# First head's attention laid beside the last pair of expert value heads

## The chip, the cores and the metric

The kernel runs on one core of a Trainium2 chip. The metric is device time in microseconds (us). The kernel before takes 1966.53 us (median of 3 runs, 1964.88 to 1967.22). The engines are TensorE (PE; its weight loads are PEld), VectorE (DVE), ScalarE (ACT), GpSimd (POOL) and SyncE (SP), which here only issues DMAs.

## The reference

Two layers on x of 32 sequences of 100 tokens and 256 channels (3200 tokens). The first is a gated cross-attention. The second, which the change touches, is a Switch-head layer: 8 heads, and in each 8 experts for the values and 8 for the output, of which a token uses 2.

```python
q = jnp.einsum('bsd,hpd->bhsp', x, q_w.reshape(H, P, D))
k = jnp.einsum('bsd,hpd->bhsp', x, k_w.reshape(H, P, D))
xv = jnp.einsum('bsd,hedp->bshep', x, v_w.reshape(H, E, D, P))
v = jnp.einsum('bshep,bshe->bhsp', xv, gate_v)
att = jax.nn.softmax(jnp.einsum('bhqp,bhkp->bhqk', q, k) * SCALE, axis=-1)
ctx = jnp.einsum('bhqk,bhkp->bqhp', att, v)
weighted = ctx[:, :, :, None, :] * gate_o[..., None]
out = jnp.einsum('bshep,hepd->bsd', weighted, o_w.reshape(H, E, P, D))
```

H = 8 heads, E = 8 experts, P = 128 channels of a head, D = 256, attention within each sequence of 100 tokens. Everything is float32; the kernel makes the large products from float16 high and low parts (hi·hi, hi·lo, lo·hi), so that each takes three matmuls.

## The kernel before, in words

Three stages follow each other: queries, cross-attention, and the expert stage (from about 600 us on), which is one block of programs, one for each engine. Engines run their own lists in order and meet at semaphores. The expert stage has four phases.

**Gates and q, k.** The layer-normalised x is turned and split into `xhi`, `xlo`; the gates are computed; q and k of all heads are written to the DRAM tensor `qk` (until about 757 us).

**Values.** Four pairs of heads, 25 tiles of 128 tokens each, two units (`unit`, one for each head of the pair) per tile: 200 units. A unit is 12 matmuls of 512 columns (L1226) in two halves of 6, each half into one bank of `e_pv`. VectorE gates and sums the first half (four operations at L1104 and L1108, then the sum `e_dsum` at L1115), ScalarE gates the second half (four operations, L1165), GpSimd adds it all (L994, L998, L1002) into `e_out`. TensorE may fill a half's bank again when the unit before last has been read: `s_ds` for the first half, `s_av` for the second. SyncE stores five tiles at a time to the DRAM tensor `v` (L954). The last stores are waited for at L967.

**Attention of head 0 alone** (`attention_alone`). A group is 4 sequences, 400 tokens; a head has 8. For group b: scores (TensorE, L1599), maxima (VectorE, L1465, L1469), exponentials (ScalarE, L1548), reciprocal (L1475), normalisation (GpSimd, L1431). In the next group's turn: the turning of the weights (TensorE, L1608), its copy (VectorE, L1480), the product with v (TensorE `attend`, L1617), and the split of the result into `a_chi` (ScalarE, L1555) and `a_clo` (VectorE, L1484). In the same phase SyncE loads the output weights of head 0 in four pieces (L1381), x1 into `o_main` (L1385), q, k and v of each group (L1362, L1363, L1373); ScalarE and VectorE split the pieces (`piece`, L1581 and L1517), GpSimd clears `o_side` (L1455).

**Heads** (`heads`). Output tiles of head h (L1637: 12 matmuls of 512 columns each, three tiles to a group, a 25th tile at a head's end) lie beside the attention groups of head h+1. So group 8 here is the first group of head 1, beside the first three output tiles of head 0. Within a group TensorE does scores of b, the turning of b-1, a tile, `attend` of b-1, two tiles. Behind the first group of each two, one weight piece of the next head is split: ScalarE waits there for the DMA of the piece (`o_wst`), VectorE for ScalarE. SyncE's loop loads, for each two groups, q and k of the next, v, again q, k, v, and then one piece.

```python
def attention_alone(eng, group, piece=lambda h, buf, jj: None):
    for jj in range(2):
        group(fixed(jj), ())
        piece(0, 0, 2 * jj)
        piece(0, 0, 2 * jj + 1)
    with eng.Fori(1, NGR // 2) as jj:
        group(Batch(2 * jj, 0, jj), ())
        group(Batch(2 * jj + 1, 1, jj), ())
```

Of the kernel before, what the change touches and what calls it, by code (L numbers as in the profile page):

```python
# [29 lines left out]
P = 128  # L30
# [842 lines left out]
def stage_experts_in(nc, k, sems, big, mv, sel_t, q_t, k_t, v_t, rs, qk_out, v_out):  # L873


    with ExitStack() as ctx:
# [6 lines left out]
        xhi, xlo = (m.sbuf(f"e_x{n}", [P, DC, T], F16) for n in ("hi", "lo"))  # L883
        std, rstd, half = (m.sbuf(n, [SQ, NB]) for n in ("e_std", "e_rstd", "e_half"))
        wst = m.sbuf("e_wst", [P, 2, DC, H * PD])
        sst = m.sbuf("e_sst", [P, DC, P])
        shi, slo = (m.sbuf(f"e_s{n}", [P, DC, P], F16) for n in ("hi", "lo"))
        qkhi, qklo = (m.sbuf(f"e_qk{n}", [P, DC, 2 * H * PD], F16) for n in ("hi", "lo"))
        vhi, vlo = (m.sbuf(f"e_v{n}", [P, DC, HE * PD], F16) for n in ("hi", "lo"))
# [4 lines left out]
        order = m.sbuf("e_order", [P, E])  # L894
        rsb = m.sbuf("e_rs", [P, 1])
        m1, m2, top, tot = (m.sbuf(f"e_{n}", [P, NT * 2 * H]) for n in ("m1", "m2", "top", "tot"))
# [53 lines left out]
        def sync_values(sp, between):  # L950
            def stores(i):
                for g in range(5):
                    sp.wait_ge(s_vo, 50 * i + 10 * (g + 1) + 2)
                    sp.dma_start(  # L954
                        v_out[640 * g:640 * g + 640, bass.ds(i * 2 * PD, 2 * PD)].rearrange(
                            "(t p) n -> p t n", p=P),
                        vout[:, 5 * g:5 * g + 5, :, :].rearrange("p t a d -> p t (a d)")
                    ).then_inc(s_vst[g], 16)

            with sp.Fori(0, H // 2 - 1) as i:  # L960
                stores(i)
            for g in range(5):
                sp.wait_ge(s_vst[g], 16 * 2)
            between(sp)
            stores(H // 2 - 1)
            for g in range(5):
                sp.wait_ge(s_vst[g], 16 * (1 + H // 2))  # L967

        def gpsimd(pool):
# [35 lines left out]
            with pool.Fori(0, H // 2) as i:  # L1005
                for g in range(5):
                    pool.wait_ge(s_vst[g], 16 * i + 16)
                    pass_wait(pool, s_pass)
                    with pool.Fori(5 * g, 5 * g + 5) as t:
                        unit(i, g, t, 0)  # L1010
                        unit(i, g, t, 1)

        def vector(dve):
# [67 lines left out]
            for h in range(H):  # L1081
                cut = slice(h * E * PD, (h + 1) * E * PD)
                dve.wait_ge(s_vw[h % 2], 16 * (h // 2 + 1))
                dve.tensor_scalar(vhi[:, :, cut], wst[:, h % 2, :, :], WS, None,
                                  ALU.mult).then_inc(s_vhi, 1)
                dve.wait_ge(s_vhi, h + 1)
                dve.scalar_tensor_tensor(out=vlo[:, :, cut], in0=wst[:, h % 2, :, :], scalar=WS,
                                         in1=vhi[:, :, cut], op0=ALU.mult,
                                         op1=ALU.subtract).then_inc(s_vlo, 1)
# [28 lines left out]
            with dve.Fori(0, H // 2) as i:  # L1118
                with dve.Fori(0, NT) as t:
                    unit(i, t, 0)  # L1120
                    unit(i, t, 1)

        def scalar(act):
# [44 lines left out]
            with act.Fori(0, H // 2) as i:  # L1168
                with act.Fori(0, NT) as t:
                    unit(i, t, 0)  # L1170
                    unit(i, t, 1)

        def tensor(pe):
# [42 lines left out]
            def unit(i, t, hh):  # L1216
                n = 50 * i + 2 * t + hh
                for half in range(2):
# [4 lines left out]
                    col = 2 * E * PD * i + E * PD * hh + half * 512  # L1223
                    for j, (c, a, b) in enumerate((c, a, b) for c in range(DC)
                                                  for a, b in ((xhi, vhi), (xhi, vlo), (xlo, vhi))):
                        last = pe.matmul(p_v[:, hh, half, :], a[:, c, bass.ds(t * P, P)],  # L1226
                                         b[:, c, bass.ds(col, 512)], start=j == 0, stop=j == 3 * DC - 1)
                    last.then_inc(s_vp, 1)

            with pe.Fori(0, H // 2) as i:  # L1230
# [3 lines left out]

        programs = Programs()
        programs.sync, programs.sync_values, programs.gpsimd = sync, sync_values, gpsimd
        programs.vector, programs.scalar, programs.tensor = vector, scalar, tensor
        programs.s_gates = s_go
# [3 lines left out]
def stage_attention_out(nc, k, sems, experts, x1, qk, v, o_w, y):  # L1242
# [42 lines left out]
    def attention_alone(eng, group, piece=lambda h, buf, jj: None):  # L1285

        for jj in range(2):
# [42 lines left out]
    with ExitStack() as ctx:  # L1330
# [45 lines left out]
        def sync_second(sp):  # L1376
            load_v(sp, fixed(0))
# [415 lines left out]
```

## Time and profile before

| quantity | value |
|---|---|
| median of 3 runs | 1966.53 us |
| the profiled execution's own time | 1965.53 us |
| its span, first to last instruction | 1963.7 us |
| busy: TensorE, VectorE, ScalarE, GpSimd | 96%, 77%, 58%, 48% of the span |
| last expert matmul starts | 1276.14 us |
| first output matmul (L1637) starts | 1325.92 us |

A busy share is the union of an engine's instructions over the span. Matmuls overlap in the records: their starts, not their lengths, tell how fast they follow one another. The granted clock is the share of TensorE's full clock, 2.4 GHz, that it had; 0.5 is 1.2 GHz. A line of a timeline has start, length, engine, line, operation, output and inputs, count, and in square brackets the idle time ahead of it with what ended it.

### The profile page before, as it was taken

How to read it: one execution, taken by the hardware profiler on the slowest of the kernel's cores; microseconds unless marked ns; L12 is line 12 of the kernel's file. 1: busy time of each engine (PE TensorE's matmuls, PEld its weight loads, DVE VectorE, ACT ScalarE, POOL GpSimd, SP SyncE). 2: the span in 40 equal slices, each digit the busy share in tenths (PEclk: the TensorE clock that was granted, in tenths of full speed). 3: DMA queues.
4: the chain of work that ended last, by engine and by line, in shares of the span. 5: the costliest groups of instructions: out<-in, count | busy, mean ns of one | idle time of the engine just before them, and what ended most of it. 6: DMA issues, size and time to landing. Idle time of an engine off the chain costs nothing. (4 is left out here: it accounts for less than half of the span.)

```text
span 1963.7 us, 59110 instructions
## 1 busy us (share of the span) xinstructions
PE 1885.1 (96%) x13454; PEld 1154.2 (59%) x13454; DVE 1503.7 (77%) x4285; ACT 1138.9 (58%) x3588; POOL 933.8 (48%) x1361
## 2 busy tenths in 40 slices
PE   5899999999997999999999999959999999999998
PEld 2678888888875554444444444455555555555543
DVE  6688898888987943555555555538999999999989
ACT  3688888888885444444444444435555555555543
POOL 4122222222212003666666666626677766766767
PEclk9999999999998999999999999969999999999999
DMA  3777888788752483000000000063222222222202
GB/s 123 145 115 117 118 119 120 119 119 121 119 80 104 204 332 130 27 27 27 27 27 27 27 24 20 27 191 91 72 78 72 68 83 66 79 73 76 76 10 68
DMA packets 192136, 174.08 MB, mean 89 GB/s; under 512 B 51921, under 2 KB 183378, under 8 KB 190034
## 3 DMA queue, kind: packets, MB, share of 16 engines
q1 hardware_dynamic: 189906, 165.06, 37.0%
q0 software_dynamic: 2176, 8.39, 1.2%
q8 instruction: 23, 0.38, 0.1%
q14 instruction: 31, 0.25, 0.1%
HBM read 112.41 MB, written 60.98 MB: 88 GB/s over the span
## 5 line engine op out<-in xcount | busy, mean ns | idle before, releaser
L1442 POOL TENSOR_TENSOR o_side<-o_side,o_tmp 128x256 f32 (+1 forms) x528 | 398.4, 755 | 193.0 <-POOL o_side L1442 73.3
L1165 ACT ACTIVATE big<-e_pv,gates 128x128 f32<-128x128 f32 x800 | 228.7, 369 | 291.4 <-PE e_pv L1226 289.9
L640 ACT ACTIVATE c_ex<-c_sm,c_nmax 100x361 f32<-100x361 f32 x512 | 302.6, 593 | 55.5 <-DVE c_nmax L523 50.1
L1565 ACT ACTIVATE o_tmp<-o_py,gates 128x256 f32<-128x256 f32 x528 | 222.3, 475 | 191.9 <-PE o_py L1637 141.4
L1637 PE MATMUL o_py<-o_whi,a_chi 128*128 128x512 f16 x800 | 304.1, 380 | 0.4 <-DVE o_side L1498 0.2
L1226 PE MATMUL e_pv<-e_vhi,e_xhi 128*128 x800 | 303.2, 379 | 1.2 <-ACT e_out L1155 1.2
L1637 PE MATMUL o_py<-o_wlo,a_chi 128*128 128x512 f16 x800 | 303.5, 379 | 0.0
L1637 PE MATMUL o_py<-o_whi,a_clo 128*128 128x512 f16 x800 | 303.4, 379 | 0.0
L1226 PE MATMUL e_pv<-e_vlo,e_xhi 128*128 x800 | 303.2, 379 | 0.0
L1226 PE MATMUL e_pv<-e_vhi,e_xlo 128*128 x800 | 303.2, 379 | 0.0
L1104 DVE TENSOR_SCALAR e_acc<-e_pv,gates 128x128 f32<-128x128 f32 x400 | 121.8, 346 | 236.3 <-PE e_pv L1226 236.3
L523 DVE CUSTOM_DVE_ANT_0 c_sm<-c_ps,c_mbias 100x361 f32<-100x361 f32 x512 | 268.6, 526 | 39.9 <-PE c_ps L725 33.0
L1498 DVE SCALAR_TENSOR_TENSOR o_main<-o_py,gates,o_main 128x256 f32 (+1 forms) x536 | 256.0, 478 | 36.1 <-issue 20.8
L1498 DVE SCALAR_TENSOR_TENSOR o_side<-o_py,gates,o_side 128x256 f32 (+1 forms) x536 | 254.0, 474 | 0.0
L732 PE MATMUL c_pt<-ident,c_ex 100*121 100x100 f32 x1536 | 244.8, 268 | 3.6 <-ACT c_ex L640 1.8
L732 PEld LDWEIGHTS c_pt<-ident,c_ex 100*121 100x121 f32 x1536 | 215.3, 185 | 28.7 <-DVE c_ext L533 6.8
L994 POOL TENSOR_TENSOR big<-big 128x256 f32<-128x256 f32 x200 | 145.1, 726 | 159.2 <-ACT big L1165 112.7
L479 POOL TENSOR_SCALAR c_mbias<-c_mraw 100x361 f32<-100x361 uint8 x32 | 15.9, 497 | 391.2 <-DMA c_mraw<-in_mask 239.8
L725 PE MATMUL c_ps<-c_kst,c_qst 128*100 128x361 f16 x512 | 171.9, 336 | 7.5 <-DVE c_nmax L523 2.8
L533 DVE COPY c_ext<-c_pt 121x300 f32<-121x300 f32 x320 | 148.4, 464 | 8.1 <-PE c_pt L732 7.2
L1548 ACT ACTIVATE a_ex<-a_ps,a_mxs 100x100 f32<-100x100 f32 x256 | 84.8, 343 | 110.6 <-DVE a_mxs L1469 110.6
L1226 PEld LDWEIGHTS e_pv<-e_vhi,e_xhi 128*128 x800 | 78.3, 98 | 95.9 <-issue 1.6
(166 smaller groups left out, 3392.4 us busy)
## 6 DMA issues: line engine op xcount, KB each, us to landing
qk<-e_out SPq DMA_DIRECT2D x16, 1600.0 KB, 5.2
c_kst<-k_parts SPq DMA_DIRECT2D x256, 90.2 KB, 4.9
a_q<-qk SPq DMA_DIRECT2D x64, 200.0 KB, 2.4
a_k<-qk SPq DMA_DIRECT2D x64, 200.0 KB, 2.5
v<-e_out SPq DMA_DIRECT2D x20, 640.0 KB, 3.3
a_v<-v SPq DMA_DIRECT2D x64, 200.0 KB
c_ctx<-in_ctx_t SPq DMA_DIRECT2D x32, 361.0 KB, 3.4
e_wst<-in_v_w POOLq DMA_DIRECT2D x8, 1024.0 KB, 7.8
```

What stands on the lines that cost most here:

```text
L523: dve.tensor_tensor_reduce(out=sm[:, h % 4, :], in0=p_s[0:SQ, h % 2, 0:SK], in1=mbias[:, b.par, :], scale=-0.25 / WS, scalar=BIG, op0=ALU. ...
L533: dve.tensor_copy(ext[:, h % RING, :], p_t[0:KW, h % 2, 0:KC * SQ]).then_inc(s_extd, 1)
L640: act.activation(ex[:, h % 4, 0:SK], sm[:, h % 4, :], ACT.Exp, scale=-1.0, bias=nmax[:, h % 4:h % 4 + 1], accum_out=den[:, b.par, HEAD[h]: ...
L725: pe.matmul(p_s[0:SQ, h % 2, 0:SK], qst[:, b.par, HEAD[h], :], kst[:, b.par, HEAD[h] // 2, :], start=True, stop=True).then_inc(s_s, 1)
L732: last = pe.transpose(p_t[0:KW, h % 2, c * SQ:(c + 1) * SQ], ex[:, h % 4, c * KW:(c + 1) * KW], k.ident[0:SQ, 0:SQ])
L994: pool.tensor_tensor(tsum[:, hh, :, :], tmp[:, hh, 0:2, :], tmp[:, hh, 2:4, :], ALU.add).then_inc(s_ts, 1)
L1165: act.activation(tmp[:, hh, e, :], p_v[:, hh, 1, e * PD:(e + 1) * PD], ACT.Copy, scale=gate).then_inc(s_av, 1)
L1226: last = pe.matmul(p_v[:, hh, half, :], a[:, c, bass.ds(t * P, P)], b[:, c, bass.ds(col, 512)], start=j == 0, stop=j == 3 * DC - 1)
L1442: pool.tensor_tensor(side[:, x.t, :], side[:, x.t, :], tmp[:, slot(x, r), j, :], ALU.add).then_inc(s_pool, 1)
L1498: dve.scalar_tensor_tensor(out=into[:, x.t, :], in0=p_y[:, q, j, :], scalar=gate, in1=into[:, x.t, :], op0=ALU.mult, op1=ALU.add).then_inc ...
L1565: act.activation(tmp[:, slot(x, r), j, :], p_y[:, q, j, :], ACT.Copy, scale=gate).then_inc(s_av, 1)
L1637: last = pe.matmul(p_y[:, q, :, :].rearrange("p j d -> p (j d)"), a[:, bass.ds(buf * T + x.t * P, P)], b[:, buf, cut], start=j == 0, stop= ...
```

## The change

Every engine's program of the expert stage runs only three of the four pairs in its loop. The fourth is handed out as `last_pair(t)`, one tile's two units, written out without a loop. `first_head` takes the place of `attention_alone`: it lays three of these tiles into each of the 8 groups of head 0, in the places where the heads have output tiles, and tile 24 behind them. The value weights stand in one tensor `e_vw`, hi and lo of two heads together, so that the pairs that are done free room; `o_main`, `o_side` and others are placed over dead tensors. The pieces of head 0's output weights are loaded ahead of the values, x1 in the last pair. GpSimd clears `o_side` in eight parts. Ahead of the heads TensorE waits until VectorE and ScalarE have read the last unit. SyncE issues the last stores among the groups' loads, and waits for the last one ahead of the loads of head 1.

```diff
-            with pe.Fori(0, H // 2) as i:
+            with pe.Fori(0, H // 2 - 1) as i:
                 with pe.Fori(0, NT) as t:
                     unit(i, t, 0)
                     unit(i, t, 1)
 
+            def last_pair(t):
+                unit(H // 2 - 1, t, 0)
+                unit(H // 2 - 1, t, 1)
+
+            return last_pair
...
-    def attention_alone(eng, group, piece=lambda h, buf, jj: None):
-
-        for jj in range(2):
-            group(fixed(jj), ())
-            piece(0, 0, 2 * jj)
-            piece(0, 0, 2 * jj + 1)
-        with eng.Fori(1, NGR // 2) as jj:
-            group(Batch(2 * jj, 0, jj), ())
-            group(Batch(2 * jj + 1, 1, jj), ())
+    def first_head(eng, group, last_pair, piece=lambda h, buf, jj: None):
+
+        for b in range(NGR):
+            group(fixed(b), [(lambda t=t: last_pair(t)) for t in range(TT * b, TT * b + TT)])
+            if b < 2:
+                piece(0, 0, 2 * b)
+                piece(0, 0, 2 * b + 1)
+        last_pair(NT - 1)
...
         def sync_first(sp):
             load_qk(sp, fixed(0))
             load_qk(sp, fixed(1))
+            for jj in range(PIECES):
+                load_piece(sp, 0, jj)
...
+            load_v(sp, fixed(0))
+            load_v(sp, fixed(1))
             load_qk(sp, fixed(2))
-            load_v(sp, fixed(1))
-            load_x1(0)
-            load_x1(1)
-            with sp.Fori(1, NGR // 2) as jj:
-                groups(0, jj)
-                load_x1(jj + 1)
+            for g in range(5):
+                load_x1(g)
+            stored = 0
+            for b in range(2, NGR):
+                load_qk(sp, fixed(b + 1))
+                load_v(sp, fixed(b))
+                while 5 * (stored + 1) < TT * b + 1:
+                    store_values(stored)
+                    stored += 1
+            while stored < 5:
+                store_values(stored)
+                stored += 1
+            for g in range(5):
+                sp.wait_ge(experts.s_values_stored[g], 16 * (1 + H // 2))
             with sp.Fori(1, H - 1) as h:
...
-            def clear(h, buf, jj):
-                if jj == 2:
-                    pool.memset(side[:, :, :], 0.0).then_inc(s_pool, POOL_AHEAD)
-
-            attention_alone(pool, group, clear)
+            CLEARED = TT * (NGR - 1)
+
+            def beside(t):
+                last_pair(t)
+                if t % TT == 1 and t < CLEARED:
+                    pool.memset(side[:, t - 1:t - 1 + TT, :], 0.0).then_inc(s_clear, 1)
+
+            first_head(pool, group, beside)
+            pool.memset(side[:, CLEARED:NT, :], 0.0).then_inc(s_pool, POOL_AHEAD)
...
-            attention_alone(pe, group)
+            first_head(pe, group, last_pair)
+            pe.wait_ge(experts.s_gated_dve, 2 + NT * H)
+            pe.wait_ge(experts.s_gated_act, 8 + 4 * NT * H)
             heads(pe, group, tile, lambda h, buf, jj: None, rest)
```

How the instructions stand on TensorE, from the end of the value loop into head 0. Before (`a_ps` are scores, `a_pt` the turned weights, `a_pc` the product with v):

```order
L1231 COMPARE_AND_BRANCH
L1230 REGISTER_ALU
L1230 COMPARE_AND_BRANCH
L1599 MATMUL a_ps<-a_k,a_q 100x100 x8
L1608 MATMUL a_pt<-ident,a_ex 100x100 x4
L1617 MATMUL a_pc<-a_ext,a_v 128x100 x4
L1291 UNCONDITIONAL_BRANCH
```

Now, the start of a middle group (`e_vw` are the value weights; two units follow, then `a_pc`):

```order
L1637 MATMUL a_ps<-a_k,a_q 100x100 x4
L1646 MATMUL a_pt<-ident,a_ex 100x100 x4
L1244 MATMUL e_pv<-e_vw,e_xhi 128x512 x2
L1244 MATMUL e_pv<-e_vw,e_xlo 128x512
...
L1655 MATMUL a_pc<-a_ext,a_v 128x100 x4
```

The scores of a group stand ahead of its first tile and `attend` of the group before stands behind it; 72 expert matmuls now lie between one group's scores and the next's, where there were none.

How TensorE goes over into the heads now. The branch carries the two new waits:

```order
L1244 MATMUL e_pv<-e_vw,e_xlo 128x512
L1349 UNCONDITIONAL_BRANCH [waits e_s_av,e_s_ds]
L1341 UNCONDITIONAL_BRANCH
L1341 ISA
L53 ISA [waits a_s_k_0,a_s_q_0]
L1637 MATMUL a_ps<-a_k,a_q 100x100 [waits a_s_ex]
```

Scores of group 8 stand behind tile 24 of the last pair and behind both waits; before, scores of group 8 stood behind `attend` of group 6.

SyncE's queue at the same place, before (the last five stores, then everything for head 0):

```order
L1373 DMA a_v<-v 100x4x128 [waits e_s_vst_3,e_s_vst_4,e_s_vst_2,e_s_vst_0,e_s_vst_1]
L954 DMA v<-e_out 128x5x256 [waits e_s_vo] x5
L1381 DMA o_wst<-in_o_w 128x512 [waits e_s_vst_3,e_s_vst_2,e_s_vst_4,e_s_vst_1,e_s_vst_0]
L1381 DMA o_wst<-in_o_w 128x512 x3
L1362 DMA a_q<-qk 128x400 [waits a_s_s]
L1363 DMA a_k<-qk 128x400
L1373 DMA a_v<-v 100x4x128
L1385 DMA o_main<-x 128x5x256 x2
```

and now (the last two stores, the wait for all, then the loop of head 1 with its first piece `o_wst` behind q, k, v, q, k, v):

```order
L955 DMA v<-e_out 128x5x256 [waits e_s_vo] x2
L1444 UNCONDITIONAL_BRANCH [waits e_s_vst_3,e_s_vst_2,e_s_vst_4,e_s_vst_1,e_s_vst_0]
...
L1388 DMA a_q<-qk 128x400
...
L1389 DMA a_k<-qk 128x400
...
L1392 DMA o_wst<-in_o_w 128x512
```

The wait for the last store moved from ahead of head 0's loads to ahead of head 1's.

## Rows read from the trace of the kernel before

**Rows 1.** The page, part 2: 40 slices of 49.1 us, TensorE and its granted clock.

```profile
PE   5899999999997999999999999959999999999998
...
PEclk9999999999998999999999999969999999999999
```

**Rows 2.** Busy time by engine in two stretches (windows).

```profile
core 0: us, PE busy (x) PEld busy (x) DVE busy (x) ACT busy (x) POOL busy (x), PEclk, DMA share, GB/s
1275.00:1300.00 25.00, 7.83 (x48) 6.33 (x45) 9.60 (x20) 8.32 (x28) 10.29 (x9) 0.61 0.60 186
1300.00:1325.00 25.00, 20.01 (x115) 18.46 (x116) 10.13 (x28) 11.51 (x54) 5.06 (x7) 0.64 0.59 181
```

**Rows 3.** Timeline of TensorE, last expert matmuls to scores of group 10.

```profile
1262.11 0.38 PE L1226 MATMUL e_pv<-e_vhi,e_xhi 128*128 x1
...
1276.14 0.38 PE L1226 MATMUL e_pv<-e_vhi,e_xlo 128*128 x1
1276.35 1.57 PE L1599 MATMUL a_ps<-a_k,a_q 128*100 128x100 f32 x16
1281.79 0.90 PE L1608 MATMUL a_pt<-ident,a_ex 100*100 100x100 f32 x4 [3.87 <-POOL a_ex L1431]
...
1335.73 0.87 PE L1599 MATMUL a_ps<-a_k,a_q 128*100 128x100 f32 x8
...
1345.83 0.34 PE L1599 MATMUL a_ps<-a_k,a_q 128*100 128x100 f32 x2
```

**Rows 4.** Timeline of TensorE, one full group in the heads.

```profile
1407.04 0.87 PE L1599 MATMUL a_ps<-a_k,a_q 128*100 128x100 f32 x8
1407.74 0.51 PE L1608 MATMUL a_pt<-ident,a_ex 100*100 100x100 f32 x4
...
1416.73 0.87 PE L1599 MATMUL a_ps<-a_k,a_q 128*100 128x100 f32 x8
```

**Rows 5.** Timeline of VectorE, an expert unit of the last tile.

```profile
1275.46 0.61 DVE L1104 TENSOR_SCALAR e_acc<-e_pv,gates 128x128 f32<-128x128 f32 x2 [0.98 <-PE e_pv L1226]
...
1276.76 0.29 DVE L1115 TENSOR_TENSOR e_dsum<-e_acc 128x128 f32<-128x128 f32 x1
```

**Rows 6.** Timeline of ScalarE, the last expert unit.

```profile
1276.72 1.14 ACT L1165 ACTIVATE big<-e_pv,gates 128x128 f32<-128x128 f32 x4 [1.35 <-PE e_pv L1226]
```

**Rows 7.** Timeline of GpSimd, last expert units, first normalisation, clearing of side.

```profile
1276.98 0.46 POOL L1002 TENSOR_TENSOR e_out<-e_tsum,e_dsum 128x128 f32 x1 [0.18 <-POOL e_tsum L998]
...
1279.46 0.45 POOL L1002 TENSOR_TENSOR e_out<-e_tsum,e_dsum 128x128 f32 x1 [0.18 <-POOL e_tsum L998]
1280.88 0.85 POOL L1431 TENSOR_TENSOR a_ex<-a_ex,a_rsum 100x400 f32<-100x400 f32 x1 [0.97 <-DVE a_rsum L1475]
...
1294.64 5.43 POOL L1455 MEMSET o_side<- 128x6400 f32 x1
```

**Rows 8.** Timeline of the DMA issues on SyncE's queue.

```profile
1279.94 0.37 SPq L954 DMA_DIRECT2D v<-e_out  x1
1283.63 1.78 SPq L1381 DMA_DIRECT2D o_wst<-in_o_w  x4
...
1331.01 0.31 SPq L1373 DMA_DIRECT2D a_v<-v  x1
1331.80 0.35 SPq L1381 DMA_DIRECT2D o_wst<-in_o_w  x1
```

**Rows 9.** DMA issues in the heads: count, size, us from issue to landing.

```profile
a_k<-qk SPq DMA_DIRECT2D x45, 200.0 KB, 2.4
o_wst<-in_o_w SPq DMA_DIRECT2D x24, 256.0 KB, 3.1
```

**Rows 10.** Timeline of ScalarE, the first weight piece of head 1.

```profile
1336.29 0.63 ACT L1581 ACTIVATE o_whi<-o_wst  x1
```

**Rows 11.** Timeline of VectorE behind that piece.

```profile
1338.48 0.58 DVE L1480 COPY a_ext<-a_pt 100x400 f32<-100x400 f32 x1
```

**Rows 12.** Timeline of TensorE, the attention product it waits for.

```profile
1339.37 1.03 PE L1617 MATMUL a_pc<-a_ext,a_v 100*128 100x100 f32 x8
```

More of the change, by code:

```diff
@@ L948, in sync, with sync_values, store @@
             sp.wait_ge(s_vlo, H)
-        def sync_values(sp, between):
-            def stores(i):
-                for g in range(5):
[L953 to L961, printed above, removed]
+        def sync_values(sp):
+            def store(i, g):
+                sp.wait_ge(s_vo, 50 * i + 10 * (g + 1) + 2)
+                sp.dma_start(
+                    v_out[640 * g:640 * g + 640, bass.ds(i * 2 * PD, 2 * PD)].rearrange(
+                        "(t p) n -> p t n", p=P),
+                    vout[:, 5 * g:5 * g + 5, :, :].rearrange("p t a d -> p t (a d)")
+                ).then_inc(s_vst[g], 16)
+            with sp.Fori(0, H // 2 - 1) as i:
+                for g in range(5):
+                    store(i, g)
             for g in range(5):
                 sp.wait_ge(s_vst[g], 16 * 2)
[L964 to L967, printed above, removed]
+            return lambda g: store(H // 2 - 1, g)
         def gpsimd(pool):
@@ L1011, in gpsimd @@
                         unit(i, g, t, 1)
+            def last_pair(t):
+                if t % 5 == 0:
+                    pool.wait_ge(s_vst[t // 5], 16 * (H // 2))
+                unit(H // 2 - 1, t // 5, t, 0)
+                unit(H // 2 - 1, t // 5, t, 1)
+            return last_pair
         def vector(dve):
@@ L1171, in scalar, with last_pair @@
                     unit(i, t, 1)
+            def last_pair(t):
+                unit(H // 2 - 1, t, 0)
+                unit(H // 2 - 1, t, 1)
+            return last_pair
         def tensor(pe):
@@ L1233, in tensor, with last_pair @@
                     unit(i, t, 1)
+            def last_pair(t):
+                unit(H // 2 - 1, t, 0)
+                unit(H // 2 - 1, t, 1)
+            return last_pair
         programs = Programs()
@@ L1519, in piece @@
                                          op1=ALU.subtract).then_inc(s_wlo, 1)
-            attention_alone(dve, group, piece)
+            first_head(dve, group, last_pair, piece)
             dve.wait_ge(s_g, 1)
+            dve.wait_ge(s_clear, NGR - 1)
             dve.wait_ge(s_x, 80)
@@ L1581, in piece @@
                 act.activation(whi[:, buf, cut], wst[:, cut], ACT.Copy, scale=WS).then_inc(s_whi, 1)
-            attention_alone(act, group, piece)
+            first_head(act, group, last_pair, piece)
             act.wait_ge(s_g, 1)
@@ L1590, in scalar, with tensor @@
             heads(act, group, tile, piece, rest)
-        def tensor(pe):
+        def tensor(pe, last_pair):
             def scores(b):
```

91 lines of the change are left out of this document (44 added, 47 removed).

## The prediction

> **What bounds the kernel now.** I read the page's 40 slices first. TensorE has a 9 nearly everywhere; the dip that lies in the expert stage is slice 26, with a 5 and a granted clock of 6 [rows 1]. The table by windows puts it between 1275 and 1325 us: TensorE is busy for 7.83 and 20.01 of 25 us, at 0.61 and 0.64 of its clock [rows 2]. That is the attention of head 0, alone. On both sides TensorE is the bound: 65 expert matmuls start between 1262.11 and 1276.14, one each 0.2158 us without a gap [rows 3], and in the heads two groups start 9.69 us apart [rows 4], of which 36 output matmuls at 0.2158 are 7.77. So the time of a change here is read on TensorE, from the first scores at 1276.35 to a point that both kernels pass in the same state. I take the scores of group 10 at 1345.83: 69.48 us, by way of group 9 at 1335.73 [rows 3]. In it lies the work of head 0's attention and of six output tiles.
>
> **What the attention costs beside other work.** A group in the heads is 9.69 − 7.77 = 1.92 us of TensorE: scores 0.70 (1407.04 to 1407.74), turning and product with v 1.22 together [rows 4]. Before the heads begin, the changed kernel has 8 scores and 7 of the other two beside the last pair: 8·0.70 + 7·1.22 = 14.1 us. Then the waits must be covered.
> TensorE may run ahead by a unit, as each half has its own bank. Of 2.59 us for a unit (12·0.2158), VectorE needs 1.6 (1275.46 to 1276.76 + 0.29) and idled 0.98 ahead of it [rows 5]; ScalarE needs 1.14 and idled 1.35 [rows 6]. A group adds to VectorE a maximum and a copy (0.58 for the copy, [rows 11], and I take as much for the others) for some 2 us, against six units' idle time of 6·0.98 = 5.9 and the 1.92 that the group itself makes longer. It adds to GpSimd a normalisation of 0.85 us and a share of the clearing, 5.43·3/25 = 0.65 [rows 7]. To ScalarE it adds four exponentials, for which I take the 1.14 of a gating. All find room within one or two units, and a unit's lag is what the banks allow. Followed through one group, with TensorE's scores at 0: copy of the turned weights done at about 2.1, gating of the first half (ready at 2.4) by 3.9, exponentials by 3.0, second half (ready at 3.7) by 4.9; the bank is wanted again for it from 8.4 on. The load of the table for exponentials, once, and the pieces of head 0 fit too: each stands behind a whole group's room. I cost all these waits at nothing; bounds from 0 to 1.5 us for each of 8 groups (a whole unit of VectorE that TensorE waits for), so 0 to 12, and nothing below. Code without loops has fewer register instructions, but TensorE is bound by its matmuls already, so no gain there.
> VectorE's last sum of a unit ran from 1276.76 to 1277.05. A GpSimd addition started within it, at 1276.98, and took 0.46; the one at 1279.46, with no such sum beside it, took 0.45 [rows 5, 7]. So the two do not hold each other up for longer than a row shows.
> The Trainium skill, in "SBUF — State Buffer", section "Who interferes with whom", says that a VectorE instruction with two SBUF inputs and a GpSimd instruction that reads SBUF take turns, the second waiting until the first is done; a clearing, which only writes, is spared. By it the addition at 1276.98 should have waited until 1277.05, which the trace does not bear out, and a normalisation could hold up VectorE's sum once a group.
>
> **The step into the heads.** TensorE now waits for the last gating. ScalarE's ended at 1276.72 + 1.14 = 1277.86, 1.51 us after TensorE was free at 1276.35 [rows 3, 6]. With an answer of some 0.15 that is 1.65 us of idle TensorE, between 0.5 (had it been ready) and 3.0 (ScalarE a unit's work late). Then scores of group 8 to scores of group 9: 9.69. GpSimd's last part of the clearing, 5.43·4/25 = 0.87 us, starts 3.6 us after 1276.35 [rows 7] and ends at 4.4; VectorE's first output gating could start near 3.9. I cost this at nothing, as the banks of three more products lie between; bound 0.7.
>
> **The wait that is next.** SyncE issues the last store when GpSimd is done, at 1279.94, and issued the next DMA at 1283.63, its landing waited for [rows 8]. That is 7.28 us after 1276.35. Now this wait stands ahead of the loads of head 1. Counted from the scores of group 8 (1.65 later) the first of them goes out at 5.6. The piece of head 1 stands behind six other loads: the spacing between two issues that wait for nothing is 0.79 (1331.01 to 1331.80), so 4.7, and its landing takes 3.1 [rows 8, 9]: 5.6 + 4.7 + 3.1 = 13.4. ScalarE wants it 0.56 after the scores of group 9 (1336.29 against 1335.73), so at 9.69 + 0.56 = 10.25 [rows 3, 10]. It is 3.2 us late. Behind ScalarE's split stand on VectorE its own split, the maxima and the copy, which ended at 1339.06 where TensorE's product with v started at 1339.37 [rows 11, 12]: 0.3 of slack. TensorE stands still for 2.9 us in group 9, which was 10.10 long before, now 13.0. The q and k of group 9 go out at 6.4 and land 2.4 later, at 8.8, in time for 9.69. Bounds: nothing, if SyncE's issues go closer together and the piece lands with its neighbours; 5.5, if it takes 1.5 more to land and the loop 1 more to enter.
> The clock: transposes that started after an idle 3.87 us took 0.90 for four, against 0.51 at the full clock [rows 3, 4]. A halt of 2.9 may do the same to what follows. A granted clock of 0.5 over a few us costs about half of them; I take 0.5, bounds 0 and 1.7.
>
> **The sum.** 14.1 + 1.65 + 9.69 + 13.0 + 0.5 = 38.9 us, where there were 69.48. 30.5 us go. The profiled execution's own time is 1965.53, its span 1963.7 and 1.8 around it; it comes to 1935.0. The median of the runs is 1.0 above that execution: 1936.0. What stays the same: pairs one to three and heads 1 to 7, in which TensorE's order is unchanged. x1 loads beside the last pair and head 0's pieces ahead of the values, both long before anything waits for them.
>
> **Rivals.**
> 1. The piece of head 1 comes in time. Group 9 keeps its 10.10: 14.1 + 1.65 + 9.69 + 10.10 = 35.5, 34.0 go: 1932.5. For it: the landings are medians, and some issues follow each other faster. Against it: 3.2 us are a lot to find in seven issues. Chance 0.17.
> 2. Forecast, 1936, own range 1933.5 to 1940. Chance 0.60.
> 3. The last pair is not free of halts: the banks' lag of a unit is used up when a group's additions fall on VectorE, ScalarE and GpSimd together. At 1.5 us for each of 8 groups 12 more: 1948. To it belongs also, as its smaller case, that the normalisation holds up VectorE's sum for its whole length in each group: 8·0.85 = 6.8, 1943. The rule of the Trainium skill above stands for that case; I give it 0.03 of the chance here. For it: GpSimd is the last in the chain, with three additions a unit. Against it: in the heads TensorE keeps its 9.69 with the same attention beside it. Chance 0.18.
> 4. Slower. The attention's chain queues behind units: an exponential behind ScalarE's gating, the normalisation behind GpSimd's chain, the copy behind VectorE's unit; if TensorE reached the turning before this chain ended, it would wait in each group for a unit's way through three engines, from 1275.46 to 1279.91, 4.5 us [rows 5, 7]; 8·4.5 = 36: 1972. It decides from 30.5/8 = 3.8 us a group on. Against it: the turning is a whole group, 15.5 us of expert matmuls, behind the scores. Chance 0.03.
> 5. The change doesn't do what it says: head 0's work is held back by a load or a buffer until the last pair has ended, and the time stays within 0.2% (4 us, about what runs of this kernel can tell from none). Chance 0.02.
>
> **Numbers.** The likeliest is 1936. 1 to 3 together make 0.95. The range goes from just below the first rival to about the shared-access case of the third, 1931 to 1946, which leaves out most of 3's upper half and the last two, some 0.15. Faster by over 0.2%: 0.95; within: 0.02; slower: 0.03.
>
> **What would show it.** Right: in the last pair expert matmuls keep 0.2158 us apart with the attention's between; groups start 17.5 us apart (72 matmuls, 15.54, and 1.92); the granted clock is 1.00 in it; a gap of 1.65 us ahead of group 8; ScalarE idle ahead of its first split of head 1 with the DMA named, and TensorE idle for about 3 us at the product with v in group 9. Wrong: halts of TensorE at `e_pv` named after `e_dsum` or `big`; a late q or k in group 9; a group 9 as long as the others.

## The result, and the profile after

| | before | changed |
|---|---|---|
| median, us (runs) | 1965.70 (4) | 1935.82 (4) |
| lowest to highest | 1963.51 to 1967.22 | 1932.65 to 1941.85 |
| profiled execution: time / span | 1965.53 / 1963.7 | 1935.28 / 1933.5 |
| granted clock, mean | 0.984 | 0.995 |
| TensorE busy | 1885.1 | 1873.0 |

The changed kernel takes 0.9853 of the time before, with a 95% interval of 0.9837 to 0.9869. The medians are 29.9 us apart. The prediction said 1936.0, in a range of 1931 to 1946.

The page of the changed kernel, part 2, answers to [rows 1] (40 slices, of 48.3 us now):

```profile
PE   5999999999997999999999999999999999999998
...
PEclk9999999999998999999999999999999999999999
```

The dip at slice 26 is gone: TensorE has a 9 there, and so has the granted clock. The timeline of TensorE in the last pair of heads of the value experts, one group of head 0's attention:

```profile
1162.10 0.87 PE L1637 MATMUL a_ps<-a_k,a_q 128*100 128x100 f32 x8
1162.81 0.51 PE L1646 MATMUL a_pt<-ident,a_ex 100*100 100x100 f32 x4
...
1168.34 1.03 PE L1655 MATMUL a_pc<-a_ext,a_v 100*128 100x100 f32 x8
...
1179.57 0.87 PE L1637 MATMUL a_ps<-a_k,a_q 128*100 128x100 f32 x8
```

From scores to scores are 17.47 us, and the row at 1162.81 shows the full clock (0.51 for four transposes, where [rows 3] had 0.90). The granted clock from 1145.86 to 1289.69 is 1.00. No row of TensorE between 1145.86 and 1289.69 names a wait.

The timeline of TensorE from the last groups into the heads, which answers to [rows 3, 12]:

```profile
1266.88 0.87 PE L1637 MATMUL a_ps<-a_k,a_q 128*100 128x100 f32 x8
...
1289.30 0.38 PE L1244 MATMUL e_pv<-e_vw,e_xlo 128*128 128x512 f16 x1
1291.78 0.94 PE L1637 MATMUL a_ps<-a_k,a_q 128*100 128x100 f32 x8 [2.09 <-ACT big L1177]
...
1301.54 0.87 PE L1637 MATMUL a_ps<-a_k,a_q 128*100 128x100 f32 x8
...
1304.97 0.38 PE L1675 MATMUL o_py<-o_whi,a_clo 128*128 128x512 f16 x1
1308.94 1.11 PE L1655 MATMUL a_pc<-a_ext,a_v 100*128 100x100 f32 x8 [3.59 <-issue]
...
1310.46 0.62 PE L1675 MATMUL o_py<-o_whi,a_clo 128*128 128x512 f16 x1
...
1313.87 0.39 PE L1675 MATMUL o_py<-o_wlo,a_chi 128*128 128x512 f16 x1
...
1316.90 0.87 PE L1637 MATMUL a_ps<-a_k,a_q 128*100 128x100 f32 x8
```

Scores of groups 7, 8, 9 and 10 start at 1266.88, 1291.78, 1301.54 and 1316.90. A halt of 2.09 stands ahead of group 8 and one of 3.59 in group 9, ahead of `a_pc`. The output matmul at 1310.46 took 0.62, where one of this shape takes 0.38 at the full clock. From it to the one at 1313.87 are eight starts, 0.43 us apart instead of 0.2158; behind that one the spacing is 0.2158 again. In the table by windows (the columns of [rows 2]) the clock behind that halt stands between the two levels:

```profile
1310.00:1320.00 10.00, 10.00 (x47) 4.73 (x47) 8.01 (x21) 4.45 (x16) 6.14 (x9) 0.83 0.14 38
```

SyncE's issues, of that place, answer to [rows 8]: the last store, the first load of head 1, its first weight piece.

```profile
1292.75 0.40 SPq L955 DMA_DIRECT2D v<-e_out  x1
1297.00 0.37 SPq L1388 DMA_DIRECT2D a_q<-qk  x1
...
1301.45 0.35 SPq L1392 DMA_DIRECT2D o_wst<-in_o_w  x1
```

The DMA issues from 1290 to 1320 (count, size, us from issue to landing) answer to [rows 9], ScalarE's and VectorE's timelines to [rows 6, 10] and [rows 11].

```profile
o_wst<-in_o_w SPq DMA_DIRECT2D x1, 256.0 KB, 4.5
```

```profile
1289.72 1.14 ACT L1177 ACTIVATE big<-e_pv,gates 128x128 f32<-128x128 f32 x4 [1.45 <-PE e_pv L1244]
...
1306.07 0.63 ACT L1619 ACTIVATE o_whi<-o_wst  x1 [3.85 <-DMA o_wst<-in_o_w]
```

```profile
1306.97 0.69 DVE L1554 SCALAR_TENSOR_TENSOR o_wlo<-o_wst,o_whi  x1 [4.24 <-ACT o_whi L1619]
...
1308.26 0.57 DVE L1517 COPY a_ext<-a_pt 100x400 f32<-100x400 f32 x1
```

The piece lands 4.5 us after its issue; ScalarE idled 3.85 for it. Then come ScalarE's split, VectorE's split, the maxima and the copy at 1308.26, and TensorE starts `a_pc` at 1308.94.

### The profile page after: what moved, and what is told of

Read it like the earlier page. It is cut to its first block and busy times, and to the rows that moved or that the text cites. A ratio compares the mean times of both kernels' runs of the same rounds, so it can differ in the third digit from the quotient of the medians.

```text
span 1933.5 us, 57514 instructions
## 1 busy us (share of the span) xinstructions
PE 1873.0 (97%) x13454; PEld 1145.7 (59%) x13454; DVE 1503.0 (78%) x4285; ACT 1137.4 (59%) x3588; POOL 935.6 (48%) x1368
## 5 line engine op out<-in xcount | busy, mean ns | idle before, releaser
L1244 PE MATMUL e_pv<-e_vw,e_xhi 128*128 (+1 forms) x1600 | 475.9, 379 | 1.2 <-ACT e_out L1167 1.2
L1244 PE MATMUL e_pv<-e_vw,e_xlo 128*128 (+1 forms) x800 | 303.2, 379 | 0.0
L523 DVE CUSTOM_DVE_ANT_0 c_sm<-c_ps,c_mbias 100x361 f32<-100x361 f32 x512 | 268.3, 525 | 38.9 <-PE c_ps L725 32.7
L1244 PEld LDWEIGHTS e_pv<-e_vw,e_xhi 128*128 (+1 forms) x1600 | 156.5, 98 | 186.6 <-issue 1.6
L1675 PEld LDWEIGHTS o_py<-o_whi,a_clo 128*128 (+1 forms) x800 | 78.2, 98 | 95.1 <-issue 0.8
```

What stands on the lines that cost most here:

```text
L523: dve.tensor_tensor_reduce(out=sm[:, h % 4, :], in0=p_s[0:SQ, h % 2, 0:SK], in1=mbias[:, b.par, :], scale=-0.25 / WS, scalar=BIG, op0=ALU. ...
L1675: last = pe.matmul(p_y[:, q, :, :].rearrange("p j d -> p (j d)"), a[:, bass.ds(buf * T + x.t * P, P)], b[:, buf, cut], start=j == 0, stop= ...
```

## The experiments

Three sets of runs, each on one chip with its own runs of the kernel before, whose medians were 1966.77 (9 runs), 1965.51 (7) and 1963.87 (9). Kernels with one run give a trace to read and no comparison of times. I read them in the same measure: the scores of group 7 to the scores of group 10, with the three steps in it (7→8, 8→9, 9→10).

| kernel | time, us (runs) | ratio to before, 95% | 7→8 | 8→9 | 9→10 | sum |
|---|---|---|---|---|---|---|
| r_after, the changed kernel | 1939.05 (5) | 0.9854, 0.9835 to 0.9873 | 24.93 | 9.77 | 15.38 | 50.08 |
| e1_wait_later | 1933.20 (5) | 0.9829, 0.9808 to 0.9851 | 24.93 | 9.77 | 9.95 | 44.65 |
| e2_piece_first | 1934.53 (5) | 0.9829, 0.9808 to 0.9850 | 24.92 | 9.77 | 9.95 | 44.64 |
| e4_both | 1934.57 (5) | 0.9837, 0.9817 to 0.9857 | 22.64 | 10.87 | 11.18 | 44.69 |
| e3_wait_at_tile | 1936.87 (1) | | 22.64 | 10.88 | 17.14 | 50.66 |
| e5_tiles_first | 1952.74 (4) | 0.9930, 0.9908 to 0.9951 | | | | |
| e6_maxima_5 | 1950.62 (1) | | 24.90 | 9.77 | 16.43 | 51.10 |
| e6_maxima_9 | 1953.51 (1) | | 25.32 | 9.76 | 16.66 | 51.74 |
| e8_clear_apart | 1929.22 (5) | 0.9822, 0.9802 to 0.9841 | 22.64 | 10.48 | 9.78 | 42.90 |
| e7_before_placed | 1962.83 (1) | | | | | |
| e9_tile_alone | 1939.45 (1) | | 24.90 | 9.77 | 15.85 | 50.52 |
| e10_short_code | 1948.37 (1) | | 24.90 | 9.77 | 16.34 | 51.01 |

### The halt in group 9

**r_after** is the changed kernel once more, beside the next three.

> The changed kernel again, beside its variants, so that they share one chip. 1935.8 us as before (its runs spread from 1932.7 to 1941.9). Scores of group 8 to scores of group 9: 9.8 us, of group 9 to group 10: 15.4 us, as in its first trace.

1939.05 against 1966.77: 27.7 us less, and the same two halts (2.12 and 3.62).

**e1_wait_later**: SyncE issues head 1's first loads and its first weight piece ahead of the wait for the last store.

```diff
+            groups(1, 0)
+            weights(1, 0)
             for g in range(5):
                 sp.wait_ge(experts.s_values_stored[g], 16 * (1 + H // 2))
+            with sp.Fori(1, NGR // 2) as jj:
+                groups(1, jj)
+                weights(1, jj)
-            with sp.Fori(1, H - 1) as h:
+            with sp.Fori(2, H - 1) as h:
```

> SyncE waits for the last value stores behind the loads of groups 9 and 10 and the first weight piece of head 1, not ahead of them. My theory (that wait makes the piece late, ScalarE waits for it 3.9 us, and TensorE stands for 3.6 us in group 9 and runs at half clock behind it): the piece goes out behind the v of group 9, some 5.7 us after the scores of group 8, lands by 9.8 at the latest, ScalarE does not wait, group 9 takes 10.1 instead of 15.4 us: 5.3 us less, about 1930.5. Rival (the halt is TensorE's own, at the end of straight code into the loop, or VectorE's backlog from the switch): group 9 stays near 15 us and the time near 1936.

TensorE's scores of groups 9 and 10, then ScalarE's split of the piece, which now names no wait:

```profile
1302.11 0.87 PE L1642 MATMUL a_ps<-a_k,a_q 128*100 128x100 f32 x8
...
1312.06 0.87 PE L1642 MATMUL a_ps<-a_k,a_q 128*100 128x100 f32 x8
```

```profile
1302.67 0.63 ACT L1624 ACTIVATE o_whi<-o_wst  x1
```

Group 9 takes 9.95 instead of 15.38; 5.43 less in the trace, 5.85 in the medians. The slowest run of this kernel, 1937.49, is below the fastest of the changed one, 1937.70.

**e2_piece_first**: the loads and the wait stay, only the weight piece goes ahead of the last store.

```diff
-            while stored < 5:
+            while stored < 4:
                 store_values(stored)
                 stored += 1
+            weights(1, 0)
+            store_values(4)
             for g in range(5):
                 sp.wait_ge(experts.s_values_stored[g], 16 * (1 + H // 2))
+            groups(1, 0)
...
```

> Only the first weight piece of head 1 is issued ahead of the last value store; the wait for the store still stands ahead of all q, k and v of head 1. If the piece alone makes the halt, as I say: group 9 takes 10.1 us, 5.3 us less than the changed kernel, about 1930.5, the same as with the wait moved. If it is a late q, k or v of groups 8 and 9: TensorE still halts in group 9, for up to 3.6 us, now named after a DMA.

Group 9 takes 9.95 again. So q, k and v were in time, and the piece alone made the halt, as the prediction had it.

What the halt costs is 5.43 and not the 3.59 of its row. Counted between starts it is 3.75 (1304.97 + 0.2158 to 1308.94). The lower clock behind it costs 1.9: `a_pc` is followed after 1.08 instead of 0.87, and the eight spacings up to 1313.87 take 3.41 instead of 1.73. Group 9 of e1 has a gap of some 0.2 of its own, which the changed kernel lacks. VectorE's backlog costs nothing more: up to 1316.90 no row of TensorE behind the halt names a wait.

### The halt ahead of group 8

**e3_wait_at_tile**: TensorE waits for the last gatings only ahead of the first output tile, where the products' banks are wanted, so that group 8's scores don't wait.

```diff
-            pe.wait_ge(experts.s_gated_dve, 2 + NT * H)
-            pe.wait_ge(experts.s_gated_act, 8 + 4 * NT * H)
             heads(pe, group, tile, lambda h, buf, jj: None, rest)
...
                 if x.place == 0:
+                    pe.wait_ge(experts.s_gated_dve, 2 + NT * H)
+                    pe.wait_ge(experts.s_gated_act, 8 + 4 * NT * H)
                     pe.wait_ge(s_wlo, PIECES * (h + 1))
```

> TensorE's two waits for the last gating stand ahead of the first output tile, not ahead of the scores of group 8; nothing else. From the start of the last expert matmul to the start of the first output matmul the changed kernel took 3.6 us (1289.30 to 1292.90). If the gap is the wait for ScalarE: scores and turning run in it, and the output matmul starts some 0.2 to 0.9 us after ScalarE's gating ends, 2.5 us in all: 1.1 less. If it is the step into the loop: the scores start about 0.9 us after the last expert matmul has ended and nothing stops the tile: about as much. The halt in group 9 gets longer by what is gained here, since the store's landing has not moved: the sum to the scores of group 10, and the time, stay as they are (1936).

```profile
1290.46 0.87 PE L1637 MATMUL a_ps<-a_k,a_q 128*100 128x100 f32 x8
...
1292.30 0.39 PE L1677 MATMUL o_py<-o_whi,a_chi 128*128 128x512 f16 x1 [0.62 <-issue]
...
1301.34 0.87 PE L1637 MATMUL a_ps<-a_k,a_q 128*100 128x100 f32 x8
...
1310.04 2.00 PE L1655 MATMUL a_pc<-a_ext,a_v 100*128 100x100 f32 x8 [4.90 <-issue]
...
1318.48 0.87 PE L1637 MATMUL a_ps<-a_k,a_q 128*100 128x100 f32 x8
```

7→8 is 2.29 shorter, and 0.62 of it comes back as a halt at the first output matmul (1292.30). But group 8 takes 1.1 longer and group 9 takes 17.14, with a halt of 4.90: what TensorE gains ahead of a wait for a landing it hands over to that wait. The sum is 50.66 against 50.08.

**e4_both** has e1's and e3's edits together. It was meant to keep a late piece from taking the gain.

> The wait for the value stores behind the first loads of head 1, and TensorE's two waits for the last gating moved from ahead of the scores of group 8 to ahead of the first output tile. The first part gives 5.3 us, as above. The second: the changed kernel's TensorE stood still for 2.1 us ahead of the scores; scores and turning (1.06 us) now run in this gap, so 1.1 us less, 6.4 in all: 1929.4. Rival for the second part: most of the 2.1 us is the step from straight code into the loop and not the wait for ScalarE, whose last gating ended 0.9 us before TensorE's scores started; then the gap stays ahead of the scores at about 1 us and the output tile follows without a further one, which gives 1.1 us as well, or less if both waits add up, down to nothing: 1930.5.

44.69, as e1's 44.65, and the medians (1934.57, 1933.20) say no more: 7→8 is 2.29 shorter, and groups 8 and 9 are 1.10 and 1.23 longer. In group 8, VectorE, then GpSimd:

```profile
1295.13 0.56 DVE L1522 COPY a_ext<-a_pt 100x400 f32<-100x400 f32 x1
1297.67 0.48 DVE L1540 SCALAR_TENSOR_TENSOR o_main<-o_py,gates,o_main 128x256 f32 x1 [1.97 <-PE o_py L1682]
```

```profile
1296.20 0.95 POOL L1499 MEMSET o_side<- 128x1024 f32 x1
```

VectorE copied for group 8 until 1295.69 and then idled 1.97 in front of its first output gating. The product that the profile names had long been there. GpSimd's last clearing of `o_side` ended at 1297.15, and the gating waits on a count of GpSimd that up to there only the clearing raises. That is the term that I had bounded with 0.7 and set to nothing: it is nothing only while TensorE waits its 2.1 us first. TensorE also halts for 0.62 ahead of its first output matmul, as in e3.

In group 9 the piece is late once more. ScalarE, then TensorE:

```profile
1305.72 0.63 ACT L1624 ACTIVATE o_whi<-o_wst  x1 [1.12 <-DMA o_wst<-in_o_w]
```

```profile
1308.59 1.11 PE L1660 MATMUL a_pc<-a_ext,a_v 100*128 100x100 f32 x8 [0.86 <-issue]
```

The piece no longer stands behind the wait for the store, but still behind the store's issue, which GpSimd's last sum releases, and behind six loads. That chain did not move when TensorE's scores came earlier.

**e8_clear_apart**: e4, and the count is raised ahead of the last clearing; VectorE waits for the clearing by itself at the second place, where it first reads that part. The first piece also goes out ahead of the last store, so both places are changed at once.

```diff
-            pool.memset(side[:, CLEARED:NT, :], 0.0).then_inc(s_pool, POOL_AHEAD)
+            pool.wait_ge(experts.s_summed, 2 + NT * H)
+            pool.sem_inc(s_pool, POOL_AHEAD)
+            pool.memset(side[:, CLEARED:NT, :], 0.0).then_inc(s_clear, 1)
...
                 dve.wait_ge(s_pool, 2 * (x.act + len(ACT_PAIRS[x.place])))
+                if x.place == 1:
+                    dve.wait_ge(s_clear, NGR)
```

> Moving TensorE's waits to the tile gained nothing before: scores of group 8 came 2.3 us earlier (22.64 instead of 24.93 us after those of group 7), but groups 8 and 9 took 10.87 and 11.18 us instead of 9.77 and 9.95. My theory: VectorE's first output gating waited for GpSimd's last clearing (ended 1297.15, gating from 1297.67, VectorE idle for 1.97), and the weight piece stood behind loads that wait for the same GpSimd chain. Here GpSimd tells the others that its last sum is done ahead of that clearing instead of behind it, VectorE waits for the clearing one tile later, and the piece goes out ahead of the last store. Then groups 8 and 9 take 9.8 to 10.0 us each, 22.64 stays: 42.5 us from group 7 to group 10, where the kernel with the wait moved alone took 44.65 and the changed kernel 50.1. Time 1931. Rival: the step is bound by VectorE's own order of work and not by the clearing: groups 8 and 9 keep 22.0 us together, 44.7, time 1933 to 1935.

GpSimd, then VectorE's first output gating:

```profile
1295.10 0.45 POOL L1001 TENSOR_TENSOR e_out<-e_tsum,e_dsum 128x128 f32<-128x128 f32 x1
1295.70 0.95 POOL L1503 MEMSET o_side<- 128x1024 f32 x1 [0.15 <-POOL e_out L1001]
```

```profile
1296.11 0.48 DVE L1546 SCALAR_TENSOR_TENSOR o_main<-o_py,gates,o_main 128x256 f32 x1 [1.12 <-PE o_py L1688]
```

The gating now starts behind GpSimd's last sum (1295.55) and no longer behind the clearing (1296.65). The stretch takes 42.90, where e1 had 44.65 and the changed kernel 50.08. Against e4, group 8 is 0.39 shorter and group 9 1.40. In group 9 ScalarE's split names no wait for the piece any more, and TensorE has no halt. No run has one of the two edits without the other, so what the clearing is worth is read from group 8 alone. There the halt of 0.62 at the first output matmul stays, and group 8 takes 10.48, not the 9.8 to 10.0 that I expected. In the traces this is the shortest version: 34.7 us below the kernel before on its chip, where the changed one was 27.7 below on its own. The two weren't timed beside each other, and their intervals overlap a little (0.9802 to 0.9841, 0.9835 to 0.9873); e8 against e1 rests on the traces alone.

### Where the gain comes from

**e5_tiles_first** runs all 25 tiles of the last pair ahead of head 0's groups: loads, pieces and clearing are placed about as in the changed kernel, but nothing lies beside the attention. (Its five stores and the loads of x1 stand ahead of group 2's loads.)

```diff
-        for b in range(NGR):
-            group(fixed(b), [(lambda t=t: last_pair(t)) for t in range(TT * b, TT * b + TT)])
+        for t in range(NT):
+            last_pair(t)
+        for b in range(NGR):
+            group(fixed(b), ())
...
```

> All 25 tiles of the last pair run ahead of head 0's 8 groups, which so are alone again; everything else is as in the changed kernel: weight pieces ahead of the values, x1 and all stores beside the last pair or right behind it, buffers, clearing in parts. My theory: the gain is that head 0's chain has TensorE's expert matmuls beside it. Alone, a group takes 4.75 us, as between 1304.95 and 1319.39 before, and the first two 2.5 more for the pieces: some 41 us for head 0 where the kernel before took 49.6 (it also waited for its pieces and loads), and no halt in group 9, as the stores have landed by then. So 8.6 us less than before: 1957. Rival: the gain comes from loads and clearing that are off the way, not from the overlap: then the time is near the changed kernel's, 1936 to 1940.

TensorE's scores of groups 0, 6, 7 and 10:

```profile
1279.37 1.57 PE L1641 MATMUL a_ps<-a_k,a_q 128*100 128x100 f32 x16
...
1307.68 1.54 PE L1641 MATMUL a_ps<-a_k,a_q 128*100 128x100 f32 x8
...
1312.41 1.54 PE L1641 MATMUL a_ps<-a_k,a_q 128*100 128x100 f32 x8
...
1336.53 0.87 PE L1641 MATMUL a_ps<-a_k,a_q 128*100 128x100 f32 x8
```

Groups start 4.73 apart, as they did before. From group 0 to group 10 are 57.16 us, where the kernel before had 69.48 and the changed one, without its 25 tiles, 41.6. So 12.3 of the 27.9 us that go here come from head 0's loads, pieces and clearing being out of the way, and 15.6 from the overlap, less what the overlap itself cost (the halt in group 9, 5.4, which e5 doesn't have). Of the 12.3, 11.4 lie between the scores of groups 0 and 3 (25.66 before, 14.26 here). There TensorE of the kernel before stood longest:

```profile
1292.73 2.00 PE L1617 MATMUL a_pc<-a_ext,a_v 100*128 100x100 f32 x8 [10.03 <-DVE a_ext L1480]
```

In e5 the halt at this product is 1.50. Which of the loads, the pieces and the clearing gives how much was not taken apart. I had expected 8.6 for the first part; the rival, that it is all of it, is refuted. The overlap with late loads wasn't tried.

### How much room there was

**e6_maxima_5** and **e6_maxima_9** have VectorE take the maxima of each of head 0's groups 4 and 8 times more, into a spare tile of 512 and 1024 bytes a partition, which nothing reads.

```diff
+                for r in range(4 if isinstance(b.n, int) and b.n < NGR else 0):
+                    dve.tensor_reduce(out=k.more[:, b.n, r, :], in_=p_s[0:SQ, b.par, 0:GC].rearrange(
+                        "p (i s) -> p i s", i=GB), axis=AX, op=ALU.max)
                 dve.tensor_reduce(out=mx[:, b.par, :], in_=p_s[0:SQ, b.par, 0:GC].rearrange(
```

> VectorE takes the maxima of each of head 0's groups four more times into a spare tile (4 of 0.57 us, 2.1 us with their overlap; nothing is left out). It measures how much room the last pair has. I counted that TensorE wants the bank of a unit again some 3 us after VectorE has done with it: 2.1 us more on VectorE are taken up, groups stay 17.46 us apart, time 1936. If the room is less than I say (the prediction's third rival): groups get longer, up to 19.6, the time up to 1953.

> The same with eight more maxima, 4.3 us on VectorE in each of head 0's 8 groups. Now the copy of the turned weights comes at about 6.4 us after the scores started, and TensorE wants it at 6.2; the first unit's gating ends at 7.9, and TensorE wants its bank at 7.1. I expect TensorE to halt for 0.8 to 1.5 us a group: groups 18.5 us apart, the time 8 more, 1944. If the room is larger: 17.46 and 1936. If there was none: 21.7 and 1970.

TensorE in the last pair, with 4 more, then with 8 more:

```profile
1170.12 1.11 PE L1658 MATMUL a_pc<-a_ext,a_v 100*128 100x100 f32 x8 [0.40 <-DVE a_ext L1520]
1171.45 0.60 PE L1244 MATMUL e_pv<-e_vw,e_xhi 128*128 128x512 f16 x2 [0.22 <-DVE e_dsum L1121]
...
1188.57 1.11 PE L1658 MATMUL a_pc<-a_ext,a_v 100*128 100x100 f32 x8 [0.36 <-issue]
```

```profile
1154.30 0.60 PE L1244 MATMUL e_pv<-e_vw,e_xhi 128*128 128x512 f16 x2 [0.97 <-DVE e_dsum L1121]
...
1173.39 1.10 PE L1658 MATMUL a_pc<-a_ext,a_v 100*128 100x100 f32 x8 [2.33 <-DVE a_ext L1520]
```

One such maximum takes 0.56, four in a row 2.02, eight 3.94. With 4 more the groups start 16.24, 18.50, 18.86 and then four times 17.46 us apart: the second and third, which also have the weight pieces of head 0, pay 1.0 and 1.4, the others nothing. With 8 more they are 17.38, 20.42, 20.43, 17.86, 18.22, 17.86, 17.86, less than the 18.5 each that I had expected for the plain ones. The room on VectorE in a plain group lies between 2.0 and 3.9 us, in one with pieces below 2.0; ScalarE and GpSimd were given no more work. The kernel doesn't need it, but it is what rival 3 was about, and the mechanism is there: the rows name `e_dsum` and `a_ext` with 0.97 and 2.33.

But the time rose by more than these groups give. In both, one group in the second and one in the third round of the heads' outer loop are long: 15.69 and 14.32 with 4 more, 13.38 and 11.71 with 8 more, where the others take 9.69. The next two ask what makes those.

**e9_tile_alone** has the spare tile and nothing else; **e10_short_code** has the tile and, for the maxima, 32 short memsets on VectorE (4 a group).

```diff
+    k.more = m.sbuf("more", [SQ, 8, 4, 4])
...
+                for r in range(4 if isinstance(b.n, int) and b.n < NGR else 0):
+                    dve.memset(k.more[:, b.n, r, :], 0.0)
```

> The changed kernel with the spare tile of the doubled maxima (512 bytes in each partition, ahead of all others) and no instruction more. With four more maxima in each group, the heads had two groups of 15.7 and 14.3 us (instead of 9.7), at the second and third round of the heads' outer loop, VectorE idle 3.5 us ahead of its maxima with nothing named. If the shifted buffers do it: the same two groups here, time about 1948. If VectorE's longer program does it (the loop starts 32 instructions later): all groups 9.7, time 1936 to 1939.

> The changed kernel with the spare tile and 32 short VectorE instructions (clearings of 4 values, 0.06 us each) at the places of the 32 added maxima: VectorE's program is as long as with them, its work is not. If the place of the loop in VectorE's program makes the two long groups: 15.7 and 14.3 us again, some 10 us in all, 1948, while the groups of head 0 stay at 17.46. If VectorE's load in the last pair does it: no long group, 1936 to 1939.

e9: no long group, 1939.45. e10: head 0's groups stay at 17.46, and the two long groups are back, 15.74 and 14.14: 10.5 more than twice 9.69. VectorE's timeline at the first of them, and its waits from 1320 us on (line waited for: us, times, longest):

```profile
1464.89 0.57 DVE L1504 TENSOR_REDUCE a_mx<-a_ps 100x4 f32<-100x400 f32 x1 [3.44 <-issue]
```

```profile
DVE a_mx L1504 <- issue: 6.8, 2, 3.4
```

The DMA queue q14, which brings instructions (packets, bytes in MB, share), from 1330 to 1900 us, in e9 and then in e10:

```profile
q14 instruction: 8, 0.07, 0.0%
```

```profile
q14 instruction: 18, 0.15, 0.1%
```

Two of e10's packets fall between 1459.97 and 1464.89, the stretch of the first idle time, and two between 1626.46 and 1631.32, that of the second. In e9 none falls between 1455 and 1470 or between 1615 and 1635, where it passes the same places. So it is neither the tile nor the time of the work, but 32 more instructions on VectorE, and instructions are fetched while VectorE idles.

**e7_before_placed** is the kernel before with the output stage's buffers in the changed kernel's order.

```diff
+        wst = m.sbuf("o_wst", [P, E * D])
+        tmp = m.sbuf("o_tmp", [P, ACT_TURN, 2, D])
         chi, clo = (m.sbuf(f"a_c{n}", [P, 2 * T], F16) for n in ("hi", "lo"))
+        whi, wlo = (m.sbuf(f"o_w{n}", [P, 2, E * D], F16) for n in ("hi", "lo"))
         main = m.sbuf("o_main", [P, NT, D])
         side = m.sbuf("o_side", [P, NT, D])
-        wst = m.sbuf("o_wst", [P, E * D])
-        whi, wlo = (m.sbuf(f"o_w{n}", [P, 2, E * D], F16) for n in ("hi", "lo"))
-        tmp = m.sbuf("o_tmp", [P, ACT_TURN, 2, D])
```

> The kernel before, with only the buffers of the heads laid in the changed kernel's order (o_wst and o_tmp ahead of a_chi, the split weights ahead of o_main). Before, every second group of head 1, 3, 5 took 9.84 us in the trace; in the changed kernel 9.74: about 1.1 us over the heads. If that comes from the place of the buffers: 9.74 here, and 1.1 us less than before. If it comes from where the loop's code stands or from the order of SyncE's loads: 9.84 stays, and so the time of 1965.5.

It asks for a small thing: in several heads every second group takes 9.84 before and 9.74 after, some 1.1 us in all. With the buffers moved it stays 9.84. The buffers' place isn't the cause; what is stays open.

## Why the prediction was right

**The stretch.** The sum said 38.9 us from group 0 to group 10 (without the 25 tiles); it took 1316.90 − 1145.86 − 25·24·0.2158 = 41.6. The 2.6 us by steps:
- *The last pair*, 17.46 a group: 17.46 measured, over the seven groups 0.02 off. The steps that cost VectorE's, ScalarE's and GpSimd's additions at nothing were right. e6_maxima_5 shows VectorE with 2 us to spare in a plain group and with less in the two that have pieces.
- *The step into the heads*: 24.90 for 24.29. The mechanism was right (ScalarE's last gating). It ended at 1290.86, 1.34 after TensorE was free (1289.30 + 0.2158), earlier than the 1.51 that I took; but TensorE answered 0.92 later, not 0.15. The answer is the term that was mis-sized: a guess with no row behind it. The wait stands on a branch between two pieces of code; with the waits at the first output tile (e3, e4, e8) the answer took 0.49 to 0.50.
- *8→9*: 9.76 for 9.69.
- *Group 9*: 15.36 for 13.5. The halt was 3.59 for 2.9, since the piece landed in 4.5 instead of the heads' median of 3.1, though it went out earlier than I said (9.67 after the scores of group 8, not 10.3). And the lower clock behind the halt cost 1.9 and not 0.5, beyond my own bound of 1.7; the mean clock of 0.83 over 10 us says the same (0.17·10 = 1.7). The 10.10 for the rest of the group was 0.4 too long: 15.36 less 3.75 and 1.9 leaves 9.7.

**The rest.** The stretch gave 27.9, the spans differ by 30.2. Of the 2.3, 1.0 is the start of the values (758.35 before, 757.36 after; 755.4 to 762.0 over all traces, so chance), and 1.1 the heads' second groups. That the median came within 0.2 us of 1936.0 is thus partly luck: two misses of opposite sign, and a median of four runs that lie 9 us apart. With r_after, on its chip, the difference was 27.7, as the stretch says.

**The rivals.** 1 (the piece in time) didn't occur; e1 shows what it would have brought, 5.4, where I had 3.5. 3 didn't occur: no halt names `e_dsum` or `big` in the last pair; but its small case is half true, below. 4 and 5 didn't occur.

**What the prediction didn't ask.** It took the gain as a whole. e5 splits it: 12.3 us would have come without laying anything beside anything.

## What to carry to other kernels

When two stages are laid beside each other, look for what now stands first behind the joint: here a wait for a store, moved ahead of the next head's loads, cost 5.4 us of the gain, and hoisting one DMA issue over it brought them back. A halt costs more than its row: add the stretch at the lower clock behind it (here 1.9 for a halt of 3.6). And when a halt is taken away, measure the sum of the groups behind it and not the halt, since the next wait (a landing, a count raised by unrelated work) may have been hidden by it.

## What the runs showed of the hardware

**The place of a loop in an engine's program.** 32 short instructions more on VectorE, long before the heads, cost 10.5 us in the heads: VectorE idled 3.4 us twice with nothing named, at the two returns of the heads' outer loop, and q14 moved 18 packets instead of 8. The Trainium skill, "Runtime: NRT & Kernel Launch", section "Instruction fetch mechanics", says that a taken branch to code outside the window that the sequencer holds forces a fetch before the engine goes on. These runs agree: packets of q14 fall into both idle times, and none at these places in e9. They give it a price of 3.4 us of the engine, up to 6 of the group. Which place is good wasn't worked out.

**VectorE and GpSimd.** The changed kernel's last pair, GpSimd's normalisation, then VectorE's sums of two units:

```profile
1241.36 0.85 POOL L1464 TENSOR_TENSOR a_ex<-a_ex,a_rsum 100x400 f32<-100x400 f32 x1
```

```profile
1238.31 0.29 DVE L1121 TENSOR_TENSOR e_dsum<-e_acc 128x128 f32<-128x128 f32 x1
...
1241.77 0.59 DVE L1121 TENSOR_TENSOR e_dsum<-e_acc 128x128 f32<-128x128 f32 x1
```

and the same with 4 more maxima:

```profile
1227.86 0.85 POOL L1464 TENSOR_TENSOR a_ex<-a_ex,a_rsum 100x400 f32<-100x400 f32 x1
```

```profile
1227.96 0.90 DVE L1121 TENSOR_TENSOR e_dsum<-e_acc 128x128 f32<-128x128 f32 x1
```

VectorE's sum of two SBUF inputs takes 0.29 by itself. Started at 1241.77 beside a normalisation that ended at 1242.21, it took 0.59; started 0.10 after the start of one that ended at 1228.71, it took 0.90 and ended at 1228.86. Both sums ended 0.15 after GpSimd's instruction, so they stood until GpSimd was done. It shows the other way round too: the addition of GpSimd at 1244.40, beside VectorE's sum of 1244.36, took 0.56 instead of 0.45. The prediction held against this an addition that overlapped a sum by 0.07, too little to show it. By the rule cited there ("SBUF — State Buffer", "Who interferes with whom", in the Trainium skill) the two take turns, and here the trace agrees. It cost TensorE nothing, as VectorE idles about 1 us a unit.

**The landing of a DMA** of 256 KB was 4.5 us behind six loads of 200 KB that were issued in the 4.5 us ahead of it, 3.1 (median) in the heads.

**The answer to a semaphore** ahead of a branch: TensorE started 0.92 us after the end of the gating that it waited for. With the wait at the first output tile it started 0.50 after it (e3, 1291.80 to 1292.30). What makes the difference stays open.
